# Four message-passing layers on one core: fewer columns in the node products, layer 3's operations in another order, skip rows in transfers of four tiles

## The reference

```
h = max(layernorm(x), 0)
s, v = h[:, :64], h[:, 64:].reshape(N, 32, 3)
skip_s, skip_v = s @ W_skip0, v x W_skip1
s, v           = s @ W_nl0,   v x W_nl1              # rows that the edges read
w  = relu(edge_feature @ W_fc1) @ W_fc2               # 64 -> 64 -> 224 per edge
tp = products of w with s[dst], v[dst] and the edge's direction   # 480 per edge
agg = segment_sum(tp, src) / 32                       # 96 scalars, 128 vectors of three
out_s, out_v = agg_s @ W_out_s + skip_s, agg_v x W_out_v + skip_v
x = x + [silu(out_s[:, :64]), sigmoid(out_s[:, 64:96]) * out_v]
```

## Time and profile before

| | us |
|---|---|
| median of 3 runs | 5998.29 (5996.16 to 6000.24) |
| profiled execution | 5996.94, its span 5994.8 |
| sorting and tables, before layer 1's loop | 0 to 455 |
| layer 1's loop, phase(0, 1) | 455 to 1767 to 1905 |
| layer 2's loop, phase(1, 2) | 1905 to 3225 to 3424 |
| layer 3's loop, phase(2, 3) | 3424 to 4648 to 4857 |
| layer 4's loop, last phase | 4857 to 5912 to 5995 |
| busy: PE, DVE, POOL, ACT | 81%, 78%, 69%, 62% |

### The profile page before, as it was taken

One profiled execution on the slowest core, in us unless ns is written; L12 is line 12 of the kernel. 1 busy time (PEld: TensorE's weight loads), 2 busy tenths in 40 slices (PEclk: granted clock), 3 DMA queues, 4 the chain that ended last, 5 costly groups with the idle time before them and its releaser, 6 DMA issues. The chain is left out here.

```text
span 5994.8 us, 143106 instructions
## 1 busy us (share of the span) xinstructions
PE 4832.2 (81%) x37237; PEld 4213.6 (70%) x37237; DVE 4676.4 (78%) x14209; ACT 3728.3 (62%) x12996; POOL 4130.4 (69%) x4263
## 2 busy tenths in 40 slices
PE   0078787777888888888889899999999778888886
PEld 0047777777777777777777688888888657777776
DVE  9947777777777777777776499999998569999996
ACT  0046666666665666666665477777777567777774
POOL 1677777777777777777777377777776257777773
PEclk9999999999998999999999899999999879999998
DMA  6433333333333333333333233333333223333332
GB/s 196 112 83 73 75 75 75 75 76 75 75 81 80 75 75 75 76 75 75 74 82 76 81 81 82 81 80 82 81 81 73 73 71 84 83 84 84 82 79 63
DMA packets 599359, 487.97 MB, mean 81 GB/s; under 512 B 308216, under 2 KB 525558, under 8 KB 598871
## 3 DMA queue, kind: packets, MB, share of 16 engines
q0 software_dynamic: 195056, 322.11, 21.0%
q1 hardware_dynamic: 365562, 137.46, 10.1%
q10 hardware_dynamic: 38637, 27.25, 1.5%
HBM read 410.36 MB, written 75.56 MB: 81 GB/s over the span
## 5 line engine op out<-in xcount | busy, mean ns | idle before, releaser
L884 PE MATMUL PS<-WK 128*128 128x123 f32 (+1 forms) x21632 | 2714.0, 285 | 196.8 <-issue 190.0
L884 PEld LDWEIGHTS PS<-WK 128*128 128x128 f32 (+1 forms) x21632 | 2598.1, 198 | 357.9 <-issue 349.2
L1096 ACT ACTIVATE WK<-WK 128x64 f32<-128x64 f32 x9984 | 2468.7, 334 | 352.1 <-DVE WK L1550 351.5
L647 POOL DMA_INDIRECT WK<-HT,WK x2080 | 2032.4, 977 | 797.7 <-issue 706.6
L647 POOL DMA_INDIRECT ACC<-HT,WK x832 | 795.8, 957 | 253.4 <-issue 242.7
L566 POOL DMA_INDIRECT TB<-WK x718 | 720.1, 1003 | 248.3 <-issue 230.7
L1072 ACT ACTIVATE WK<-PS 100x512 f32<-100x512 f32 x420 | 247.0, 588 | 693.3 <-PE PS L850 693.2
L867 PE MATMUL PS<-F,WK 100*128 100x192 f32 x3360 | 657.6, 340 | 11.2 <-DVE WK L1568 8.8
L872 PE MATMUL PS<-F,WK 64*128 64x224 f32 (+1 forms) x3360 | 416.3, 367 | 214.6 <-ACT WK L1075 214.6
L867 PEld LDWEIGHTS PS<-F,WK 100*128 100x128 f32 x3360 | 541.4, 192 | 66.5 <-DVE WK L1568 37.4
L1538 DVE SCALAR_TENSOR_TENSOR WK<-iota,BKOA,WK 128x492 f32<-128x492 f32 x624 | 453.3, 726 | 156.8 <-PE PS L884 107.6
(11 more groups left out here) (234 smaller groups left out, 6605.7 us busy)
## 6 DMA issues: line engine op xcount, KB each, us to landing
WK<-TA SPq DMA_DIRECT2D x636, 72.0 KB, 1.9
WK<-HT,WK POOLq DMA_INDIRECT x2080
WK<-TB SPq DMA_DIRECT2D x212, 144.0 KB
WK<-in_ea SPq DMA_DIRECT2D x23, 612.0 KB
TA<-WK POOLq DMA_DIRECT2D x23, 612.0 KB, 7.9
ACC<-HT,WK POOLq DMA_INDIRECT x832
WK<-in_eb SPq DMA_DIRECT2D x400, 32.0 KB
HT<-WK ACTq DMA_DIRECT2D x153, 76.9 KB
```

The costliest lines, as they stand in the source:

```text
L647: eng.indirect_dma_start(out=GB[l][u % 4][:, t, :], out_offset=None, in_=HT[:, :], in_offset=bass.IndirectOffsetOnAxis(ap=idx[:, t, vc:vc ...
L884: m = eng.matmul(psA[q][0:ch, k * BN:(k + 1) * BN], ms[:, t, k * ch:(k + 1) * ch], OH[q][:, t, :], start=(t == 0), stop=(t == G - 1))
L1096: m = eng.activation(m4[:, t, 96 + vb * c:160 + vb * c], m4[:, t, 96:160] if l == 2 else TW[l][q][:, t, :], ACT.Copy, scale=tb[:, t, y1 + ...
```

## The change

- `mout` multiplies a chunk only with the columns of WO that its rows reach (`fed`). The first chunk keeps all columns: 160, 320, 192 and 161 for layers 1 to 4. The others get 64 (layers 1 and 4), 128 (layer 2) and 64, 64, 32 (layer 3).
- `mnode` for layer 3 makes two products of 192 columns in place of four of 64, 96, 96 and 96; WS2 gets 32 columns of zeros.
- In layers 3 and 4 the edge loop's order is another on PE and ACT (below); `tfeat` and `edge_e` run two tiles further ahead, and DVE splits layer 4's features six tiles ahead, not four. PE makes T(0) to T(5), f1(0) to f1(3) and f2(0), f2(1) before the loop.
- `skip_rows` fetches 4 node tiles at a time, into four buffers.
- Layer 4's first 8 table loads stand after every third of its first 24 pairs of stores, not ahead of all; each table slot has a semaphore of its own.
- Layer 4's node rows are evicted into buffers of their own (EV3), and DVE's first operands no longer wait for the stores.
- The scatter of TB does 166, 96 and 120 columns before layer 1, in phase(0, 1) and in phase(1, 2), where it did 174, 104 and 104.
- Several semaphores are merged, and their base counts raised from 4 to 8.

```diff
+        def fed(l, k):
+            p, ns = LAYERS[l], 96 if l == 2 else 64
+            if k == 0:
+                return 0, 161 if l == 3 else ns + 96
+            blocks = [(0, 96, 0, ns)] + [(96 + c * p["vb"], p["vb"], ns + 32 * c, 32) for c in range(3)]
+            hit = [(c, c + n) for f, m, c, n in blocks if f < (k + 1) * p["ch"] and k * p["ch"] < f + m]
+            return hit[0][0], hit[-1][1]
...
                 if l == 3:
-                    for u in range(8):
-                        load(0, u)
                     for j in range(NB):
                         store(eng, 3, j)
+                        if j % 3 == 2 and j < 24:
+                            load(0, j // 3)
...
                     eng.wait_ge(s_le, 3)
-                    skip_rows(0)
-                    skip_rows(1)
+                    for q in range(NSK):
+                        skip_rows(q)
...
-                        if j and j % SKB == 0 and j + SKB < NB:
+                        if j and j % SKB == 0 and j + (NSK - 1) * SKB < NB:
                             eng.wait_ge(s_o, j)
-                            skip_rows(j // SKB + 1)
+                            skip_rows(j // SKB + NSK - 1)
...
-                        eng.matmul(o[:, 0:64], t[0:64, 0, 0:BN], WS[2][:, 0:64], start=True, stop=True)
-                        eng.matmul(o[:, 160:256], t[0:64, 0, 0:BN], WS[2][:, 64:160], start=True, stop=True)
-                        eng.matmul(o[:, 64:160], t[0:96, 1, 0:BN], KV[2][:, 0:96], start=True, stop=True)
-                        m = eng.matmul(o[:, 256:352], t[0:96, 1, 0:BN], KV[2][:, 96:192], start=True, stop=True)
+                        eng.matmul(s2, t[0:64, 0, 0:BN], WS[2][:, :], start=True, stop=True)
+                        m = eng.matmul(v2, t[0:96, 1, 0:BN], KV[2][:, :], start=True, stop=True)
...
+                            edge_f2(i, u, 2)
+                            edge_a(i, u)
+                            edge_f2(i, u + 1, 2)
+                            tfeat(i, u, 6)
+                            tfeat(i, u + 1, 6)
+                            edge_f1(i, u, 4)
+                            edge_f1(i, u + 1, 4)
+                            edge_a(i, u + 1)
...
                     eng.wait_ge(s_xn, NB * (l + 1))
-                    for x in range(NEV):
-                        eng.wait_ge(s_hd[x], all_stored(l)[x])
                     if l == 3:
                         v(eng.memset(twf[:, 0:576], 0.0))
                         w_()
+                    else:
+                        for x in range(NEV):
+                            eng.wait_ge(s_hd[x], all_stored(l)[x])
```

More of the change, by code:

```diff
@@ L40 @@
 NMIN, NMAX = 26, 31
-assert SB0 + 2 * SLOOP + 2 * SB1 == EC and EC % CHA == 0
+assert SB0 + 2 * SLOOP + SB1 + SB2 == EC and EC % CHA == 0
 BLK, LAG = 4, 10
 PL0 = 7
-NEV, SKB = 5, 8
+NEV, SKB, NSK = 5, 4, 4
 EARLY = 38
@@ L279, in program @@
         s_oo, s_xo, s_wz, s_wo, s_ox, s_tl = (sem(n) for n in ("s_oo", "s_xo", "s_wz", "s_wo", "s_ox", "s_tl"))
-        s_sk, s_ske, s_skl = [sem(f"s_sk{i}") for i in range(2)], sem("s_ske"), sem("s_skl")
+        s_sk, s_ske, s_skl = [sem(f"s_sk{i}") for i in range(NSK)], sem("s_ske"), sem("s_skl")
         s_o, s_sg, s_hz = sem("s_o"), sem("s_sg"), sem("s_hz")
@@ L290, in __init__ @@
             def __init__(self, l):
-                self.L = [sem(f"e{l}_L{i}") for i in range(4)]
+                self.one = l == 3
+                self.L = [sem(f"e{l}_L{i}") for i in range(8 if l == 3 else 4)]
                 self.G = [sem(f"e{l}_G{i}") for i in range(4)]
@@ L294, in __init__, with landed @@
                     sem(f"e{l}_{n}") for n in ("T", "E", "F1", "S", "F2", "M", "A", "V", "D", "N"))
+            def landed(self, eng, g, i):
+                if self.one:
+                    eng.wait_ge(self.L[g % 8], i * 16 + 16 * (g // 8 + 1))
+                else:
+                    eng.wait_ge(self.L[g % 8 // 2], i * 32 + 32 * (g // 8 + 1))
         EG = [Edge(l) for l in range(4)]
@@ L508, in _ @@
                         load(i, u)
-                for u in range(4):
+                for u in range(6 if l >= 2 else 4):
                     load(n, u)
-                for u in range(4):
-                    eng.wait_ge(e.L[u], n * 32 + (32 if u < 2 else 0))
+                for u in range(8):
+                    if l == 3:
+                        eng.wait_ge(e.L[u], n * 16 + (16 if u < 6 else 0))
+                    elif u % 2 == 0:
+                        eng.wait_ge(e.L[u // 2], n * 32 + (32 if u < (6 if l == 2 else 4) else 0))
                 eng.sem_inc(s_sep, 1)
@@ L893, in _ @@
                 tfeat(0, 1, 0)
-                edge_f1(0, 0, 0)
-                edge_f1(0, 1, 0)
-                tfeat(0, 2, 0)
-                tfeat(0, 3, 0)
+                if l < 2:
+                    edge_f1(0, 0, 0)
+                    edge_f1(0, 1, 0)
+                    tfeat(0, 2, 0)
+                    tfeat(0, 3, 0)
+                else:
+                    tfeat(0, 2, 0)
+                    tfeat(0, 3, 0)
+                    edge_f1(0, 0, 0)
+                    edge_f1(0, 1, 0)
+                    tfeat(0, 4, 0)
+                    tfeat(0, 5, 0)
+                    edge_f1(0, 2, 0)
+                    edge_f1(0, 3, 0)
                 edge_f2(0, 0, 0)
@@ L1079, in _, with edge_w @@
                 edge_e(0, 0, 1)
-                edge_s(0, 0, 0)
-                edge_s(0, 0, 1)
+                if l < 2:
+                    edge_s(0, 0, 0)
+                    edge_s(0, 0, 1)
+                else:
+                    edge_s(0, 0, 0)
+                    edge_s(0, 0, 1)
+                    edge_e(0, 0, 2)
+                    edge_e(0, 0, 3)
+                def edge_w(i, u):
+                    eng.wait_ge(e.D, i * (8 * ND[l]) + (u * ND[l] + KW))
+                    eng.activation(tw[:, :, 3:5, :], tw[:, :, 0:2, :], ACT.Copy).then_inc(s_tw, 1)
                 def edge_n(i, u):
@@ L1496, in _ @@
                         w_()
-                    for u in range(4):
-                        eng.wait_ge(e.L[u // 2], 32)
+                    else:
+                        for x in range(NEV):
+                            eng.wait_ge(s_hd[x], all_stored(l)[x])
+                    for u in range(4 if l < 2 else 6):
+                        if u == 4:
+                            eng.sem_inc(s_xp, 1)
+                        if u >= 4:
+                            eng.wait_ge(e.T, u - 3)
+                        e.landed(eng, u, 0)
                         x0, x1, x2 = parts(u)
@@ L1560, in _ @@
                             kr = op(eng.tensor_tensor(tq[q], tq[q], tp[q][:, :, 2, :], ALU.add))
-                            eng.wait_ge(e.L[u4 // 2], i * 32 + (32 * ((u + 4) // 8) + 32))
-                            eng.wait_ge(e.T, i * 8 + (u + 1))
+                            e.landed(eng, u + ahead, i)
+                            eng.wait_ge(e.T, i * 8 + (u + ahead - 3))
                             k0 = op(x0())
```

163 lines of the change are left out of this document (89 added, 74 removed).

## The result

| | before | after |
|---|---|---|
| median, 10 runs each | 5997.23 us (5988.83 to 6008.95) | 6011.0 us (5998.72 to 6027.89) |
| ratio after to before | | 1.0024, 95% interval 1.0013 to 1.0035 |
| profiled execution, span, mean clock | 5996.94, 5994.8, 0.953 | 6024.52, 6022.8, 0.941 |

A forecast was written before the change was run, and what follows sets the result against it. Layer 3's loop was taken as bound by a PE-DVE chain, layer 4's by POOL, phases (1, 2) and (2, 3) by PE or store queue; terms summed to -19.5 us from 5996.94, 5977.4, so median 5979, range 5938 to 6002.

The forecast's parts named there:

- Rival 1: Narrower products in phase(1, 2) leave PE idle, half the node tiles fall to 1.2 GHz: about 5992 us, chance 0.20.
- phase(2, 3), first output: First skip transfer of 4 tiles, not two of 8, lets the first output go sooner: -9 us (-4 to -15).
- phase(2, 3), stores: Table loads among the stores +10 us; the queue's thin start takes up 3, smaller skip transfers save 5.
- The -5 for half of the stuck store: phase(2, 3): one store stuck 8.80 us beside a skip transfer; half-sized transfers save about half, with its aftermath: -5 us.
- Layer 4's start: DVE's operands and PE's start are done during the store drain, so POOL's 3.15 us wait goes: -3 us.
- Last phase: PE paces it; narrower output products save 5 us, of which DVE's two instructions per node leave -2 (0 to -5).
- The forecast's +1 at the end of layer 4: At the end of layer 4's loop, turns and f1 stand before the last aggregation: +1 us.
- the -8 that was forecast: phase(1, 2): narrower output and node products save PE time until the store queue at 2.49 us per node tile limits: -8 us.
- Layer 3's start: Two more turns and two more f1 before the first one-hot, +4 us; the first loop pair gives some 2.5 back.
- Layer 3's loop: The 0.51 us stall goes, but a chain through DVE takes 11.67 for 11.68 per pair: 0 us (-13 to +6).
- Rivals 2 and 3: Layer 3's loop: 2, stall time regained, -53 us, about 5926, chance 0.12; 3, pair grows to 12.1, +44, 6023, chance 0.12.
- The +2 at the end: At the end of layer 3's loop, turns and f1 (1.97 us) stand before the last aggregation: +2 us.

## Why the prediction was wrong

The step that failed is that fewer columns can only save PE time: "PE would need 0.4 less, but the queue at 2.47 hides it: 0 of its own" for phase(2, 3), and "of which DVE's two instructions per node leave -2" for the last phase. Both sums were made at 2.4 GHz. The runs showed in its place that the narrow products leave TensorE at 1.2 GHz: a node tile of phase(2, 3) takes PE 3.78 us for 2.44 with the wide ones, and PE, not the store queue at 2.47, sets the phase. Rival 1 had the fall of the clock, but for another reason (PE idle for a fifth of the time, where it was busy for 92%), only in half the node tiles of phase(1, 2), and priced it at 5992. One of the prediction's own signs of being wrong, a clock in the phases below that of before, came true.

- **phase(2, 3), first output**: forecast -9, measured -10.3 (37.4 to 27.2). Here the skip rows' size is only 7.0 of it by the test with eight tiles; the rest was not taken apart. With the narrow products alone, and eight tiles per transfer, it is 1.6 to 2.5 less than before (34.9 to 35.8). The Trainium skill's rule (DMA: Bandwidth & Descriptors, Rules for kernel authors) against small transfers had no price here: seven transfers became thirteen, and the phase is 11.6 us shorter with them.
- **phase(2, 3), stores**: forecast +10 for the loads, -3 and -5, so +2; measured +28.1, all of it the clock. With the old widths it is between +0.5 and -1.5 (172.1 twice and 170.1, for 171.6), and the loads count nothing: the queue that I took for full still took them up. The -5 for half of the stuck store was not tested by itself; with skip rows by eight this part is 4.7 longer.
- **Layer 4's start**: forecast -3, measured -8.2 (13.2 to 5.0), since DVE's splits, the turns and f1 all lie ahead of the first gather now (from 4851.80, the gather at 4861.81), not only POOL's 3.15.
- **Last phase**: forecast -2. With the narrow products alone, at 2.4 GHz, it takes 90.3 to 91.8, in the kernel before 94.4: there the -2 is about right. In the changed kernel the output products take 69.59 us for 43.92, 1.36 per node tile for 0.86; what follows them is some 8 us shorter (30.2 for 37.9), and the first of them starts 15.7 us behind the last one-hot for 12.5: +21. The forecast's +1 at the end of layer 4 lies in that last term, which is +2.1 to +3.5 in all changed kernels of usual speed (14.6 to 16.0). In all nine profiled executions with wide products in the last phase the clock reached 2.4 GHz, also in the six in which it fell to 1.2 within 0.5 us of the first product; of the five with narrow ones, one of them beyond its 16th tile, the four that began at 2.4 kept it, and the one in which it fell to 1.2 there never left it. What sets the clock at that place is open.
- **phase(1, 2)**: forecast -8. The first turn of layer 3 comes 6.4 earlier after layer 2's last one-hot (198.0 to 191.6). With the narrow output products alone in the kernel before it comes 8.4 earlier (189.6), more than the -8 that was forecast for these and the narrower node products together; why the whole change has less was not taken apart. A node product of 192 columns takes 0.42 to 0.49 and not 0.33. What took over is the store queue, as forecast: PE waits for ACT's eviction, ACT's stores are issued between the evictions, and their queue moves 3995 packets in the 53 us from 3257 to 3310, 3.26 us per node tile.

```profile
q10 hardware_dynamic: 3995, 2.75, 16.2%
```

```profile
3262.45 0.56 PE L774 MATMUL PS<-WS,WK 64*123 64x192 f32 x2 [0.93 <-ACT WK L1024]
3262.94 0.59 PE L775 MATMUL PS<-KV,WK 96*123 96x192 f32 x2
3263.36 1.14 PE L807 MATMUL PS<-WOA,ACC 128*123 128x320 f32 x6
3264.34 0.27 PE L760 MATMUL PS<-ident,WK 123*64 123x123 f32 x1
...
3266.67 0.65 PE L774 MATMUL PS<-WS,WK 64*123 64x192 f32 x2 [1.96 <-ACT WK L1024]
```

  The output product takes 0.98 there (3263.36 to 3264.34) for 1.64, as worked out; the idle 1.96 is what rival 1 expected, and the clock did fall in places (mean 0.86 from 3340 to 3376, where it was 1.00).
- **Layer 3's start**: forecast +4 and -2.5 given back. First turn to first one-hot is +3.4 (13.4 to 16.8); f2's wait of 5.79 is now one of 5.35 for DVE, so f2 comes 1.4 sooner behind the first one-hot (4.9 for 6.3), but the loop is no shorter for it.

```profile
3415.82 1.09 PE L861 MATMUL PS<-ident,WK 128*64 128x128 f32 x16 [2.39 <-ACT WK L1108]
...
3428.46 1.86 PE L899 MATMUL PS<-F,WK 64*128 64x224 f32 x8 [5.35 <-DVE WK L1666]
```

- **Layer 3's loop**: forecast 0, measured +0.4. The stall that went (0.51 x 104 = 53 us of PE) was on the chain before, and the chain that took over is as long, as worked out. Rivals 2 and 3 were wrong. The +2 at the end did not come: PE's first output product starts 13.7 us behind the last one-hot before and 13.8 now.
- **Scatter columns, semaphores**: no difference that can be seen, as forecast.

With the two widths put back the kernel is 0.42% faster (0.26 to 0.59%), 25 of 5993 us, where the sum said -19.5. That the two are near each other is in part luck, since the stages of that kernel are not those forecast: phase(2, 3) with layer 4's start gave -21.3 for -10, layer 4's loop -5.9 for 0, phase(0, 1) -1.1 for -4, phase(1, 2) with layer 3's start -4.0 for -6.5, and the last phase +3.2, with its widths unchanged.

The Trainium skill (TensorE: Matmul & The Clock Gate, Why this matters for your kernels) says to keep TensorE busy without a break to get the full clock. The narrow products of the last phase were 69.59 us without a gap at 0.50, and phase(2, 3) with those of layer 3 had PE busy for 198 of 215 us at 0.50. Being busy was not enough in these rows; the measurement decides.

Two things stay open: what makes the clock high or low when the last phase begins, and why phase(2, 3) loses it with narrow products while the last phase holds it. Adding useless columns at single places, to see which product counts, wasn't tried.

## What to carry to other kernels

Before cutting the columns of a product, read the granted clock of its stage and of the stages around it: here streams of narrow products stood at half the clock with PE busy for 92% and for all of the time, and cost more than the wide ones. Price such a cut at both clock levels; here the same narrow products of the last phase ran at the one in some executions and at the other in another. And when a wait on one engine is removed, work out the whole chain through the others first: here a stall of 53 us was worth nothing, and the sum of six terms from the rows of the trace said so to within 0.1 us per pair.

## What the runs showed that I had not expected

- From the first output to the gathers the narrow kernels take 199.65 to 199.71 us in five executions of three kernels; the wide ones vary from 169.2 to 174.8. This stretch, which PE alone paces at a constant clock, repeats to 0.1 us.
- A chip can be in a condition in which the same program takes half as long again (before 8964.6 and 8850.7, otherwise 5993 to 5997). It was met on two chips. In layer 3's loop of the kernel with the narrow products alone the instructions of DVE and ACT last as long as otherwise (a one-hot matrix 731 ns for 730), the products of PE longer (an aggregation product 305 ns for 271), and the packets of the largest queue 106 ns for 98. The waits of the kernel before with narrow products in layer 3's loop then name a "remote" releaser:

```profile
DVE WK L1551 <- remote: 607.2, 88, 7.0
ACT WK L1088 <- remote: 605.9, 95, 6.8
PE PS L885 <- ACT WK L1088: 591.7, 90, 6.9
```

  In that condition layer 3's pair takes 20.45 us in the old order and 17.86 in the new. That the order is the cause is not shown: layer 2's loop, whose order is the same in both, takes 1714 us in the one kernel and 1974 in the other. The cause of the condition was not found.
